# Attention of a gated two-layer block: three PSUM banks for the scores under the exponential and two for the scores under the maximum, in place of two and three

## What is computed

```python
    q = (query @ Wq).reshape(b, sq, NUM_HEADS, HEAD_DIM).transpose(0, 2, 1, 3)
    k = (key @ Wk).reshape(b, sk, NUM_KV_HEADS, HEAD_DIM).transpose(0, 2, 1, 3)
    v = (value @ Wv).reshape(b, sk, NUM_KV_HEADS, HEAD_DIM).transpose(0, 2, 1, 3)
    ...
    scores = jnp.einsum('bhqd,bhkd->bhqk', q, k) * scale
    probs = jax.nn.softmax(scores, axis=-1)
    out = jnp.einsum('bhqk,bhkd->bhqd', probs, v)
```

## Time and profile before

| What | Value |
|---|---|
| median of 3 runs | 1477.09 us (1474.74 to 1478.48) |
| profiled execution, its own time | 1477.09 us |
| its span in the trace | 1475.2 us |
| busy shares | PE 90%, DVE 56%, POOL 45%, ACT 34%, PEld 38% |
| queries' items in the trace | about 404 to 518 us |
| groups in the trace | about 527 to 1012 us |
| maxima (L1263) | 512, 682 ns mean |
| exponentials (L991) | 512, 597 ns mean |

### The profile page before, as it was taken

One profiled execution on the slowest core, in us unless ns is written; L12 is line 12 of the kernel. 1 busy time (PEld: TensorE's weight loads), 2 busy tenths in 40 slices (PEclk: granted clock), 3 DMA queues, 4 the chain that ended last, 5 costly groups with the idle time before them and its releaser, 6 DMA issues.

```text
span 1475.2 us, 19149 instructions
## 1 busy us (share of the span) xinstructions
PE 1329.2 (90%) x7145; PEld 564.8 (38%) x7224; DVE 832.3 (56%) x1460; ACT 500.7 (34%) x856; POOL 665.2 (45%) x400
## 2 busy tenths in 40 slices
PE   6696869999798779999999999988994899999998
PEld 4363644444343322222222222222552344444443
DVE  7965951243323268778877788742454356345363
ACT  3652111011101056666666676672221101011010
POOL 5008250800023246877778777875002644434330
PEclk9898879999899889999999999999996999999999
DMA  8364030200032110000010000000002534343321
GB/s 315 115 256 128 15 101 28 86 0 0 0 89 78 57 54 25 25 17 17 17 33 17 16 18 25 10 0 1 0 0 86 171 100 131 115 148 107 104 67 57
DMA packets 37598, 97.05 MB, mean 66 GB/s; under 512 B 5136, under 2 KB 15376, under 8 KB 37520
## 3 DMA queue, kind: packets, MB, share of 16 engines
q1 hardware_dynamic: 36368, 91.80, 19.1%
q10 hardware_dynamic: 1152, 4.19, 0.7%
HBM read 85.49 MB, written 10.49 MB: 65 GB/s over the span
## 4 chain that ended last, share of the span: by engine, by line
PE 76%; DVE 10%; ACT 4%; issue 4%; DMA 3%; POOL 2%; SPq 1%; ACTq 0%; DVEq 0%
PE bank L531 42%; PE bank L726 12%; PE bank L762 8%; PE bank L711 7%; ACT R L991 2%; DMA stage_w<-w_in 2%; PE bank L546 2%; PE bank L550 1%; PE bank L606 1%; POOL R L520 1%; PE bank L720 1%; DVE R L1071 1%; DVE stats L1084 1%; DVE xn L1106 1%; DMA stage_w<-wts_in 1%
## 5 line engine op out<-in xcount | busy, mean ns | idle before, releaser
L1263 DVE TENSOR_REDUCE mxp<-bank 128x1 f32<-128x512 f32 x512 | 323.9, 682 | 96.4 <-PE bank L711 96.3
L505 POOL TENSOR_TENSOR R<-R 128x2048 f32<-128x2048 f32 x64 | 290.2, 4535 | 109.0 <-ACT R L991 109.0
L991 ACT ACTIVATE R<-bank 128x512 f32<-128x512 f32 x512 | 282.9, 597 | 156.9 <-PE bank L762 155.8
L531 PE MATMUL bank<-XTh,R 128*128 128x512 bf16 x876 | 273.3, 389 | 3.3 <-DVE XTl L1165 2.3
L520 POOL TENSOR_TENSOR R<-stage_w,R 128x1024 bf16<-128x1024 f32 x64 | 142.0, 2226 | 257.7 <-DVE R L1370 257.7
L436 POOL TENSOR_TENSOR R<-stage_w,zero 128x1024 f32 (+1 forms) x36 | 71.1, 1974 | 369.7 <-DMA stage_w<-wts_in 246.5
L531 PE MATMUL bank<-R 128*128 128x512 bf16 x939 | 208.2, 379 | 5.5 <-issue 2.4
L531 PE MATMUL bank<-XTl,R 128*128 128x512 bf16 x440 | 171.6, 390 | 14.3 <-POOL R L520 13.6
L531 PEld LDWEIGHTS bank<-R 128*128 128x128 bf16 (+1 forms) x960 | 93.7, 98 | 118.2 <-issue 2.9
L726 PE MATMUL bank<-R 128*32 128x512 f32 x1024 | 138.8, 604 | 0.0
L531 PEld LDWEIGHTS bank<-XTh,R 128*128 128x128 bf16 x896 | 89.9, 100 | 127.5 <-issue 27.2
(11 more groups left out here) (173 smaller groups left out, 1504.8 us busy)
## 6 DMA issues: line engine op xcount, KB each, us to landing
stage_w<-w_in SPq DMA_DIRECT2D x64, 512.0 KB, 3.5
stage_w<-wts_in SPq DMA_DIRECT2D x36, 512.0 KB, 3.6
XTh<-ctx_nat_in SPq DMA_DIRECT2D x11, 512.0 KB, 5.3
XTh<-ctx_t_in SPq DMA_DIRECT2D x9, 512.0 KB, 5.7
X<-x_in SPq DMA_DIRECT2D x8, 512.0 KB, 8.3
q_scr<-R SPq DMA_DIRECT2D x32, 128.0 KB, 1.8
y_out<-X ACTq DMA_DIRECT2D x8, 512.0 KB, 2.6
R<-q_scr SPq DMA_DIRECT2D x30, 128.0 KB, 2.4
```

Of the source, the lines that this page charges most:

```text
L505: pool.tensor_tensor(PS[j % 2], PB[2 * j % 4], PB[2 * j % 4 + 1], ALU.add).then_inc(p_add, 1)
L531: mm = pe.matmul(o, a, m, start=first and a is ah and bs is bh, stop=last and a is al)
L991: act.activation(PB[kt % 4][:, h * S:(h + 1) * S], bank[2 + t % 2][:, :], ACT.Exp, scale=float(HD) ** -0.5).then_inc(exp_done, 1)
L1263: dve.tensor_reduce(mxp[:, m, n // 2, n % 2:n % 2 + 1], bank[s_bank[u % 3]][:, :], AX.X, ALU.max).then_inc(s_max, 1)
```

## The change

Bank 7 goes from the pass for the maximum to the pass for the exponential. A score now waits for the maximum two scores before it (it was three), and a product for the exponential waits for the exponential three turns before it (it was two). No instruction is added, removed or moved on any engine; only the banks and the counts waited for differ.

```diff
-        s_bank = (0, 1, 7)
+        s_bank = (0, 1)
+        t_bank = (2, 3, 7)
...
-                if u >= 3:
-                    pe.wait_ge(s_max, u - 2)
-                pe.matmul(bank[s_bank[u % 3]][:, :], QS[g % 3][0:96, h * S + qt * P:h * S + (qt + 1) * P],
+                if u >= 2:
+                    pe.wait_ge(s_max, u - 1)
+                pe.matmul(bank[s_bank[u % 2]][:, :], QS[g % 3][0:96, h * S + qt * P:h * S + (qt + 1) * P],
...
-                    if STEPS * g + t >= 2:
-                        pe.wait_ge(exp_done, STEPS * g + t - 1)
-                    pe.matmul(bank[2 + t % 2][:, :], KS[g % 3][0:98, kt * P:(kt + 1) * P],
+                    if STEPS * g + t >= 3:
+                        pe.wait_ge(exp_done, STEPS * g + t - 2)
+                    pe.matmul(bank[t_bank[(STEPS * g + t) % 3]][:, :], KS[g % 3][0:98, kt * P:(kt + 1) * P],
...
-                    act.activation(PB[kt % 4][:, h * S:(h + 1) * S], bank[2 + t % 2][:, :], ACT.Exp,
+                    act.activation(PB[kt % 4][:, h * S:(h + 1) * S], bank[t_bank[(STEPS * g + t) % 3]][:, :], ACT.Exp,
...
-                dve.tensor_reduce(mxp[:, m, n // 2, n % 2:n % 2 + 1], bank[s_bank[u % 3]][:, :],
+                dve.tensor_reduce(mxp[:, m, n // 2, n % 2:n % 2 + 1], bank[s_bank[u % 2]][:, :],
```

## The result

The changed kernel takes 1497.72 us (median of 4 runs, 1497.29 to 1503.72) against 1475.91 us (4 runs, 1472.42 to 1478.48), a ratio of 1.0159 with a 95% interval of 1.0125 to 1.0193. It is slower by about 22 us. The profiled execution took 1497.83 us, its span is 1496.0 us, 20.8 us more than the span before.

A forecast was written before the change was run, and what follows sets the result against it. TensorE, 90% busy, was taken as the bound, so its waits count, in items and groups. Terms 10.4 - 1.9 + 3.6 + 12.2 - 2.9 = +21.4 us on 1477.09 gave 1498.5 us, range 1486 to 1511.

The forecast's parts named there:

- Term 1: Queries' items: third score waits for the first maximum, behind the remainder, 1.74 us in each of items 4 to 9; +10.4 us.
- Term 2: Items 11 and 13: broken-up pauses may keep the clock from falling; half taken, -1.9 us, between 0 and -4.1.
- the sign: Items 11 and 13: in the changed kernel's profile their matmuls would all start 0.22 us apart.
- Term 3: Group 0: five-score blocks wait for maxima, 0.59 us longer in four blocks, less in others; +3.6 us, bounds 1.6 and 6.3.
- Term 4: Groups 1 to 14: third and fourth scores wait for maxima, +0.93 us a group; +12.2 us, bounds 7 and 17.
- Term 5: Tail from turn 24 of group 14: third exponential bank helps, GpSimd's adds limit it; -2.9 us, bounds -1 and -3.5.
- A: Items: the clock falls with ten pauses, 9 to 16 us more on items 4 to 9; 1509 to 1517 us; chance 0.12.
- The page's rule: Items: cycling through PSUM banks each iteration can pause TensorE so often that its clock swings between both levels.
- B: Groups come out even as exponentials' waits vanish: 0 to 5 us in place of 15.8; 1483 to 1488 us; chance 0.1.
- C: Groups get faster because maxima release banks soon enough that TensorE waits for neither reader; 1460 us; chance 0.03.
- D: Nothing to see: the items' wait vanishes too, as if VectorE took three maxima ahead of the remainder; chance 0.03.

The follow-up runs named there:

- two-and-two kernel: Against the changed kernel, bank 7 is used by nobody: two banks for scores, two for the exponentials; 1508.02 us, ratio 1.0214.
- the pool: Against the kernel before, each score and exponential product in the groups takes whichever of five banks is expected free first; items keep three score banks; 1456.87 us.
- the run with the tail alone: Against the kernel before, the third bank goes to the exponentials only after the last score; 1470.51 us, ratio 0.9947, then 1473.66 us, ratio 0.9976.
- the one with the last division: Against the kernel with five pooled banks, GpSimd divides group 14's outputs behind its last add in the last group; 1458.38 us, ratio 0.9867.

## Why the prediction was right

The forecast was 1498.5 us and the measured time 1497.72; against the profiled span the sum was +21.4 and is +20.8. The range and the mechanism held. That the time came within 1 us is in part luck: terms 3 and 4 were 1.8 us too low together, and the others 2.4 too high. By terms:

| Term | Predicted | In the trace | From |
|---|---|---|---|
| 1, items 4 to 9 wait | +10.4 | +10.5 | six items of 7.59 in place of 5.83 us |
| 2, the clock in items 11 and 13 | -1.9 (0 to -4.1) | -2.5 | 6.70 and 5.30 us in place of 6.62 and 7.85 |
| the rest of the items' way | 0 | -0.5 | a load 0.3 us and a turned row 0.2 us shorter, and small differences |
| 3, group 0 | +3.6 | +4.7 | 572.89 - 534.31 = 38.58 against 33.87 |
| 4, groups 1 to 14 | +12.2 | +12.9 | 13 times 31.18 against 30.19, and 0.1 |
| 5, the tail | -2.9 | -2.9 | 55.82 us to the last `total`, against 58.59, less the 0.1 |
| behind the tail | 0 | -1.2 | the projection starts 1.00 behind the last `total`, not 1.93, at the higher clock |
| ahead of the items | 0 | -0.2 | the first score at 426.85, not 427.09 |

**Term 1 was right in its place and size.** The third score starts 2.18 us after the first. Undoing this part alone starts the groups 7.6 us earlier in the trace, and moving two maxima ahead of the remainder moves the score to 1.17. Items 10 to 13 were covered by the waits for GpSimd, as foretold: of 4.19 and 4.31 us, 0.39 and 0.79 are left.

**Term 2: half was a guess, and came near by luck.** I had named both items at full clock as a sign to look for. The clock stayed up behind item 13's pause, and fell behind item 11's, so the sign was half wrong. In the two-and-two kernel, with the same items, it was the other one that fell. So the pauses alone don't decide it, and what does is not shown.

**Term 3 was mis-sized by 1.1 us.** The blocks of group 0 are as computed (3.91 against my 3.90). The first block takes 542.08 - 534.31 = 7.77 us in place of 6.55, not the +0.2 that I had put down: the clock is at its lower level for nearly all of it (0.55 over that block, 0.69 before). It is no chance of one execution: in all four profiles with two score banks in group 0 this block takes 7.77 to 8.46 us, and in all six with three, or with the pool, 6.34 to 6.65. The pause ahead of it is not the cause (9.57 us, before 9.37; between 8.99 and 9.84 in the other kernels). So the missing score bank keeps the clock low for longer there; by which steps is not shown.

**Term 4 was right block by block**, predicted 3.30, 4.36, 7.71, 3.55, 7.84, 4.36, measured 3.31, 4.36, 7.74, 3.56, 7.85, 4.36. The two-and-two kernel took the sum apart: the score bank taken away costs 1.56 us a group, the exponential bank added gives back 0.57.

**Term 5 was right**, and the run with the tail alone shows the same: 2.5 us in the trace and 3.5 in the times, not the 5 us that its blocks add up to, because GpSimd's adds become the bound. Without the clock at the start of the projection (-1.2 us, which I had not foreseen) the sum would be +22.0.

**The rivals.** A is out: with pauses of 1.58 us in each of items 4 to 9 the granted clock is 1.00. The page's rule that I had put beside it (the Trainium skill, TensorE: Matmul & The Clock Gate, "A second HAM failure mode: psum-queue depth-cycling") didn't come true in this stage: from 426.85 to 473.00 us TensorE cycled through two PSUM banks and paused in each item, and its clock stayed at 1.00. B is out by the groups' 31.18 us and by the two-and-two kernel. C would have needed a release 0.02 us after a maximum's start; it is 0.75. D is out by the items' rows. The change does what it says: ScalarE has all but left the chain. It is VectorE that took its place there.

## What to carry to other kernels

A bank belongs to whoever's release comes last. To price one bank more or less, write down for a block when each release arrives (start of the reader, its pace, the latency to the waiting engine: here 0.42, 0.60 and 0.75 us) and see which comes last, block by block; averages and busy shares say nothing on it. Look also at stages where the same buffers serve another rhythm: a third of the loss in the trace (7.5 of 20.8 us, terms 1 and 2 and what came with them) sat in a stage that a look at the groups alone would have missed, where three scores come together and their reader stands behind other work. And banks needn't belong to a user: five banks, handed out in the groups in the order in which they are expected free, gave 1.4%, where moving one from one side to the other lost 1.6%.

## What the runs showed of the hardware that was not expected

Pauses of TensorE that look alike don't cost alike. In the changed kernel, behind a pause in two pieces ahead of item 11 (1.58 and 0.39 us) the clock fell (0.77 over the item), behind nearly the same one ahead of item 13 (1.58 and 0.79) it didn't (1.00); in the two-and-two kernel, with the same pieces within 0.11 us, the two swapped. Shortening waits can lengthen the unbroken pause behind them: the profiled execution of the kernel with two maxima ahead lost its 6 us in that way and through later remainders, and the one with the last division lost its 1.85 to the clock. Both were right about their waits and gained nothing in these executions.

A ratio of 0.9947 with an interval of 0.9929 to 0.9966 over six runs was followed by 0.9976 over twelve new ones. The tail in the trace, 2.5 us shorter both times, had been the better witness. The span of a single profiled execution is not: in the first of the two it was as long as before, because other stages were longer.
